# Counting graph edges on TensorE: lanes of ten destinations in place of chunks of 125 edges

## The reference, cut to what matters

```python
src, dst: 20000 edges over N = 1250 nodes, sorted by dst; x: 1250 x 512
# first layer, with h = relu(layernorm(x)), xn = batchnorm(h)
agg = segment_sum(xn[src], dst)                      # neighbours
agg = agg / max(deg, 1)
conv_out = relu(agg @ W_conv + b_conv)
# Performer attention over the first 256 dense rows of h: q, k, v, phi(q), phi(k), kv, z
x = x + batchnorm(conv_out + attention(h) + h)
# second layer, with h = relu(layernorm(x))
agg = segment_sum(h[src], dst)
z = (1 + eps) * h + agg
h = relu(batchnorm(relu(batchnorm(z @ W1 + b1)) @ W2 + b2)); x = x + (z's input h) + h
```

## Time and profile before

| | us |
|---|---|
| median of 3 runs | 365.77 |
| lowest, highest | 365.72, 365.85 |
| span of the profiled execution | 363.9 |
| what the runs' median has beyond that span | 1.87 |
| PE busy in the span | 349.3 |
| DVE busy | 245.2 |
| ACT busy | 181.7 |
| POOL busy | 94.1 |

### The profile page before, as it was taken

How to read it: one execution, slowest core, us unless ns; L and a number is a source line. 1 busy time by engine, 2 the same in 40 slices (tenths; PEclk the granted TensorE clock), 3 DMA queues, 4 the chain that set the end, 5 groups by cost and what they waited for, 6 DMA issues and landing times.

```text
span 363.9 us, 6197 instructions
## 1 busy us (share of the span) xinstructions
PE 349.3 (96%) x2072; PEld 224.6 (62%) x2072; DVE 245.2 (67%) x666; ACT 181.7 (50%) x303; POOL 94.1 (26%) x163
## 2 busy tenths in 40 slices
PE   8999899989999999999998999999999999999994
PEld 4678655757777666767565675455555555565562
DVE  5889999998998995867996886522464453422325
ACT  0548538768477167454437766411533644233132
POOL 8132020000000000100042778722277465101100
PEclk9999999999999999999999999999999999999998
DMA  6990303300000000034900000000000000010223
GB/s 179 283 304 19 119 1 119 118 3 1 3 3 4 3 3 3 3 103 145 263 7 3 0 2 3 2 2 1 2 0 0 2 0 2 0 51 21 70 58 85
DMA packets 13539, 18.05 MB, mean 50 GB/s; under 512 B 1839, under 2 KB 6895, under 8 KB 13491
## 3 DMA queue, kind: packets, MB, share of 16 engines
q1 hardware_dynamic: 12538, 17.21, 16.3%
q10 hardware_dynamic: 953, 0.23, 0.3%
HBM read 14.88 MB, written 2.56 MB: 48 GB/s over the span
## 4 chain that ended last, share of the span: by engine, by line
PE 82%; DVE 6%; ACT 5%; issue 3%; POOL 2%; DMA 1%; DVEq 0%; SPq 0%; ACTq 0%; POOLq 0%
PE bank L1436 78%; PE bank L1466 2%; PE bank L1834 1%; POOL ln_s L491 1%; ACT hn L688 1%; PE bank L1793 1%; DVE st_row L1324 1%; ACT hh L832 1%; ACT sqr L694 1%; DMA edge<-src 1%; DVE x L1387 0%; PE bank L1647 0%; ACT hring L602 0%; DVE aggf L1344 0%; DVE hl L1305 0%
## 5 line engine op out<-in xcount | busy, mean ns | idle before, releaser
L1436 PE MATMUL bank<-AT,hh 125*128 125x400 f16 (+3 forms) x250 | 81.1, 332 | 1.0 <-DVE hl L1305 0.5
L1436 PE MATMUL bank<-AT,hl 125*128 125x400 f16 (+3 forms) x250 | 80.8, 331 | 0.0
L994 DVE TENSOR_SCALAR ring<-iota_code,code 125x250 f16<-125x250 f16 x200 | 46.1, 306 | 1.4 <-issue 1.4
L1436 PEld LDWEIGHTS bank<-AT,hh 125*128 125x128 f16 x250 | 24.1, 97 | 19.2 <-issue 1.1
L1436 PEld LDWEIGHTS bank<-AT,hl 125*128 125x128 f16 x250 | 24.2, 97 | 17.7 <-issue 0.2
L1436 PE MATMUL bank<-ring,S 125*128 125x250 f16 x200 | 33.5, 310 | 0.0
L1436 PE MATMUL bank<-a_hi,w_hi 128*128 128x400 f16 (+1 forms) x96 | 32.6, 339 | 0.0
L1436 PE MATMUL bank<-agg_hi,w_hi 128*128 128x400 f16 (+1 forms) x96 | 32.6, 339 | 0.0
L1436 PE MATMUL bank<-agg_hi,w_lo 128*128 128x400 f16 (+1 forms) x96 | 32.5, 338 | 0.0
L1436 PE MATMUL bank<-a_hi,w_lo 128*128 128x400 f16 (+1 forms) x96 | 32.5, 338 | 0.0
L1436 PE MATMUL bank<-agg_lo,w_hi 128*128 128x400 f16 (+1 forms) x96 | 32.5, 338 | 0.0
(11 more groups left out here) (236 smaller groups left out, 704.2 us busy)
## 6 DMA issues: line engine op xcount, KB each, us to landing
w_s<-w SPq DMA_DIRECT2D x4, 1024.0 KB, 5.0
x_in<-x SPq DMA_DIRECT2D x5, 448.0 KB
x<-x SPq DMA_DIRECT2D x2, 1120.0 KB
out<-x SPq DMA_DIRECT2D x6, 224.0 KB
wB<-wk SPq DMA_DIRECT2D x1, 1024.0 KB, 9.3
wA<-wq SPq DMA_DIRECT2D x1, 1024.0 KB, 14.3
wC<-w_conv SPq DMA_DIRECT2D x1, 1024.0 KB, 16.0
wB<-wv SPq DMA_DIRECT2D x1, 1024.0 KB, 6.0
```

The source lines that it names most:

```text
L994: return dve.tensor_scalar(ring[:, slot, j, a:b], iota_code[0:CH, a:b], code[:, bass.ds(c + j, 1)], float(-CODES * t), ALU.subtract, ALU.i ...
L1436: return pe.matmul(o, l, r, start=start, stop=stop, skip_group_check=True)
```

## The change

A lane is now 10 destinations (`LANE`), so there are 125 lanes and a window is five of them. A lane takes 256 edges from the granule (32 edges) in which it begins, as two products of 128 edges; its codes are 10 destinations x 10 tiles = 100. A window is ten products of 100 columns, two for each lane's own 100 columns of the bank, 1000 columns in all. The edges of every lane are put side by side at the start-up, by PE: `first` marks the row and granule in which each lane begins, and 20 products `edge16` x `first` pick the 256 edges of all 125 lanes for `dst` and `src`. DVE makes codes from them (`lane2`, `code2`), with each value written twice, side by side. The two one-hot instructions of a window read `iota_code` and such pairs. A flag `irregular` is made once in place of the ranges; where it is not 0 (a lane reaches over more than 8 granules, or `dst` is not sorted) all edges are counted again by a loop. In the given inputs the lanes have 127 to 185 edges and reach over 6 granules at most.

The edges now come in three overlapping DMAs for `dst` (SP) and three for `src` (ACT's queue), 384 edges to a row of 125 rows, after two memsets on DVE. ACT turns them to f16. `AT` is evicted with 50 destinations together, from PSUM columns ten apart. The branch for exact counts on DVE and PE (`big_r`) now hangs on the same flag.

```diff
-CH = 125
-NCH = E // CH
-G = 8
-Q = 4
+GRAN = 32
+REACH = 8
+LANE = 10
+LANES = N // LANE
+LPW = W // LANE
+CPL = T * LANE
+CODES = LPW * CPL
+CHUNKS = REACH * GRAN // P
+JOBS = LPW * CHUNKS
-SPARE = {"start": 20, "ranges": 5, "hT0": 3, "hT1": 3, "hT2": 4}
+SPARE = {"start": 14, "firsts": 10, "hT0": 3, "hT1": 3, "hT2": 4}
...
-            return banks[COUNT_BANK[t]][0:L, 0:CODES].rearrange("p (h a b) -> p h a b", h=2, a=T)
+            return banks[COUNT_BANK[t]][0:L, 0:CODES].rearrange("p (d a) -> p a d", a=T)
...
+        EDGE_LOADS = ((0, L - 2, WIDE), (L - 2, 1, 2 * EROW), (L - 1, 1, EROW))
...
         def _(act):
+            act.wait_ge(sem("s_pad"), 2)
+            for rows in EDGE_LOADS:
+                load_edges(act, 1, *rows)
+            for a, name in enumerate(("d_dst", "d_src")):
+                act.wait_ge(sem(name), 16 * len(EDGE_LOADS))
+                act.activation(edge16[:, a, :], edge[:, a, :], ACT.Copy).then_inc(sem("s_edge16"), 1)
...
-                dve.tensor_tensor(S[:, slot], iota_lane[0:CH], a, ALU.is_equal)
...
-                return dve.tensor_scalar(ring[:, slot, j, a:b], iota_code[0:CH, a:b], code[:, bass.ds(c + j, 1)],
-                                         float(-CODES * t), ALU.subtract, ALU.is_equal)
...
+            def one_hots(t):
+                if t >= 2:
+                    dve.wait_ge(sem("s_win"), t - 1)
+                jobs = slice(t * JOBS, (t + 1) * JOBS)
+                for o, n, values in ((S, P, lane2), (ring, CPL, code2)):
+                    shape = [P, JOBS, n // 2, 2]
+                    ins = dve.tensor_tensor(o[:, t % 2].rearrange("p j (q d) -> p j q d", d=2),
+                                            pairs(iota_code[:, 0:n]).unsqueeze(1).broadcast_to(shape),
+                                            values[:, jobs, :].unsqueeze(2).broadcast_to(shape), ALU.is_equal)
+                ins.then_inc(sem("s_hot"), 1)
...
                 if t + 1 < NW:
-                    first_lanes(t + 1)
+                    one_hots(t + 1)
                 if t:
                     low_counts(t - 1)
-                further_chunks(t)
-                if t + 1 < NW:
-                    first_chunks(t + 1)
-                if t + 2 < NW:
-                    load_range(t + 2)
+                further_edges(t)
...
-                if name == "RG":
-                    pe.wait_ge(sem("s_halves"), 1)
...
-            def count(ps, t, j, a, b, start, stop):
-                return mm(ps[:, a:b], S[:, t % 2, :, j], ring[:, t % 2, j, a:b], start, stop)
+            def count(ps, t, j, start, stop):
+                k = j // CHUNKS
+                return mm(ps[:, k * CPL:(k + 1) * CPL], S[:, t % 2, j, :], ring[:, t % 2, j, :], start, stop)
...
-                pe.load([out_r], win[t:t + 1, 1:2])
...
-                for n, j in enumerate(CHUNK_ORDER[:-1]):
-                    if n % Q == 0:
-                        pe.wait_ge(sem("s_hot"), G // Q * t + n // Q + 1)
-                    count(ps, t, j, *CHUNK_COLS[j], n == 0, False)
+                pe.wait_ge(sem("s_hot"), t + 1)
+                for j in range(JOBS - 1):
+                    count(ps, t, j, j % CHUNKS == 0, j % CHUNKS == CHUNKS - 1)
```

More of the change, by code:

```diff
@@ L29 @@
 HB = HID // P
-CH = 125
-NCH = E // CH
-G = 8
-Q = 4
+EROW = E // L
+GRAN = 32
+GPR = EROW // GRAN
+REACH = 8
+WIDE = (GPR - 1 + REACH) * GRAN
 W = 50
 NW = N // W
[L36 to L46, removed]
+LANE = 10
[5 more added lines that the diff above has]
+JOBS = LPW * CHUNKS
+FAR = 2
+PAD_DST = 2000
 COLS = [(0, 450), (450, 400), (850, 400)]
@@ L123, in take @@
         used[bank] += 1
-    take("codes", 2)
-    take("ranges", 3)
+    take("chosen", 2)
+    take("firsts", 3)
     for slot in SLOTS:
@@ L277, in gnn_kernel @@
         hT = place("hT", [P, FB, N], F32, 65)
-        ring = place("ring", [CH, 2, G, CODES], F16, 112.75)
-        S = place("S", [CH, 2, P, G], F16, 128.5)
+        ring = place("ring", [P, 2, JOBS, CPL], F16, 112.75)
+        S = place("S", [P, 2, JOBS, P], F16, 116.75)
+        edge = place("edge", [L, 2, WIDE], I32, 121.75)
+        lane2 = place("lane2", [P, LANES * CHUNKS, 2], F16, 124.75)
+        code2 = place("code2", [P, LANES * CHUNKS, 2], F16, 205.75)
+        below = place("below", [L, LANES, GPR + 1], F16, 125.75)
+        first = place("first", [L, GPR, P], F16, 127.25)
+        src_tile = place("src_tile", [P, CHUNKS * LANES], I32, 129)
+        code_all = place("code_all", [P, CHUNKS * LANES], F32, 130)
+        edge16 = place("edge16", [L, 2, WIDE], F16, 88)
+        fall = place("fall", [L, EROW], F16, 89.5)
+        from_row = place("from_row", [1, LANES + 1], F32, 90)
+        span_row = place("span_row", [1, LANES], F32, 90.5)
         dg = place("dg", [P, 2, MAXN], F32, 134.5)
@@ L410, in _ @@
         def _(sp):
[L411 to L415, removed]
+            sp.wait_ge(sem("s_pad"), 2)
+            for rows in EDGE_LOADS:
+                load_edges(sp, 0, *rows)
             load_x(sp, 0)
@@ L1160, in further_chunks @@
[L1160 to L1173 removed]
+            far = Own(dve, sem("own_far"))
@@ L1586, in attention @@
                         released("P")
-                        pe.load([most_r], most[0:1, 0:1])
                     ps = open_group(pe, name)
@@ new lines, in _ @@
+                pe.wait_ge(sem("s_hot"), t + 1)
+                for j in range(JOBS - 1):
+                    count(ps, t, j, j % CHUNKS == 0, j % CHUNKS == CHUNKS - 1)
+                with pe.If_lt(none_r, flag_r):
+                    count(ps, t, JOBS - 1, False, True).then_inc(sem("s_grp"), 1)
+                    mm(ps[:, 0:CODES], zeros16[0:L, 0:1].broadcast_to([L, P]), iota_code[0:L, :], True, False)
+                    far_ring = ring[0:L, t % 2].rearrange("p (j k) n -> p j (k n)", j=FAR)
+                    with pe.Fori(0, EROW // FAR):
+                        pe.reg_add(seen, seen, 1)
+                        pe.wait_ge(sem("s_hotx"), pe.snap(seen, min_val=1, max_val=1 << 20))
+                        for j in range(FAR):
+                            ins = mm(ps[:, 0:CODES], S[0:L, t % 2, j, :], far_ring[:, j, :], False, False)
+                        ins.then_inc(sem("s_grp"), 1)
+                    mm(ps[:, 0:1], ones16[0:L, :], zeros16[0:L, 0:1], False, True).then_inc(sem("s_win"), 1)
```

286 lines of the change are left out of this document (117 added, 169 removed), and 4 rows, old and new, of tables (LONE_BANKS, SLOTS).

## The result

The changed kernel takes **355.67 us** (median of 4 runs, 355.01 to 358.01), against 365.76 us for the kernel before on the same chip: a ratio of 0.9737, 95% interval 0.9707 to 0.9767, so 10.1 us less by the medians and 9.6 by the ratio. The forecast was 350.3 us, with 347.5 to 353 for its own case and 347 to 355.5 for 8 in 10, so the result lies outside both. The direction and the prices of a window's count and one-hots were right, and the loop gave somewhat more than reckoned; the start was wrong. The profiled span is 354.0 us. One run of experiment 1 (354.53 us) was a slow one, over 1.5% above the fastest of its kernel, and is left out of the figures there; with it the median is 352.29 us.

What follows compares the result with a forecast made beforehand. PE was taken to bound the kernel (busy 349.3 of 363.9 us), with ACT or DVE stretches between. Stages 0.5 + 3.3 + 0 + 3.3 + 0.7 + 7.65 = 15.5 us off 365.77 gave 350.3; own case 347.5 to 353 (0.63), 8 in 10 347 to 355.5.

Steps and rivals of the forecast that it cites:

- Stage 1: Start-up to 22.8 us: 0.5 us gained, 0.26 from dropping the `RG` products and 0.25 for everything else.
- a later start: Rival: the longer edge path makes K0 start 2 us later, giving 352.6 us; chance 0.13.
- ACT's table load: Start-up: the 1.28 us load comes with the edges' copy, no longer ahead of the first `hring`; bound 1 us gain.
- PE's count and DVE's one-hots: Per window: count 0.45 us instead of 1.17; one-hots 0.82 + 0.68 us, with overlap 1.45 instead of 2.49.
- The rule of neighbouring words: DVE one-hots: a repeated f16 pair is one word without its neighbour, so about 2.3 us a window; not taken.
- Stages 2 and 3: 22.8 to 53.5 us: 3.3 us gained, mostly DVE's one-hots; 53.5 to 59.09 us: zero, ACT works in its order.
- Stages 4 and 5: 59.09 to 78.94 us: 3.3 us gained, 0.5 of PE's idle 1.58 remaining; to 88.41 us: 0.7 from window 11.
- Stage 6: 88.41 to 160 us: windows 13 to 24 give 8.65 us, less 1.0 for ACT's `hn` and `kf`: 7.65.
- The new wait behind both one-hots: `s_lo` of t - 1 follows the one-hots of t + 1; a bank 0 count waits for it, and it just holds.
- The rival with slow one-hots: One-hots take 2.3 to 2.7 us a window on DVE: 356.9 us at the upper price, about 354 at 2.3; chance 0.14.
- the slower rival: TensorE's 2.4 GHz level comes much later, at about 38 us instead of 7: 366.6 us or more; chance 0.03.
- The split of the gain: Of PE's 18.1 us over 25 windows, 3.6 and 1 us are lost, and DVE gives back some 2.

Runs made afterwards that it cites:

- experiment 1: Changed kernel with its 123-row edge loads cut into 112 and 11 rows, same bytes: 352.04 us, ratio 0.9588.
- experiment 2: Changed kernel with its 123-row edge loads cut into 120 and 3 rows: 349.92 us, ratio 0.9594.
- experiment 5: Changed kernel with edge loads in 112 + 11 rows and POOL's clearing of `ATlo` moved behind the third row scale: 349.80 us, ratio 0.9551.
- experiment 8: Kernel of experiment 6 with the low counts of window t ahead of the one-hots of t + 1 on DVE: 352.53 us, ratio 0.9621.
- experiment 9: Kernel of experiment 6 with four extra products, 1750 columns in all, ahead of every window's ten on PE: 363.11 us, ratio 0.9922.
- experiment 10: Kernel of experiment 6 with both one-hot instructions reading one repeated f16 element instead of a repeated pair: 360.07 us, ratio 0.9842.
- experiment 6: Changed kernel with edge loads in 120 + 3 rows and POOL's clearing of `ATlo` moved behind the third row scale: 349.72 us, ratio 0.9556.
- experiment 3: Changed kernel with its 123-row edge loads cut into 119 and 4 rows: 354.35 us, ratio 0.9684.
- experiment 11: Kernel of experiment 6 with the first pair of x tiles issued by SP ahead of the edges: 352.10 us, ratio 0.9639.

## Why the prediction was right and wrong

- **Stage 1, the step that failed.** The prediction said: "I take 0.25 of gain for all this beside `RG`; bounds are 1 us of gain (table load) and 2.5 us of loss". The loss was 6.6 us. The view was the right one (the edges' landing at 3.97 us), and a later start was named as a rival, at 352.6 us and 0.13. What failed is its price: the step counted the bytes and the copies in series, and did not ask how a load of 123 rows is served, nor what a late landing does to the clock. 123 rows landed at 11.26 us where 120 took to 5.06, and about 1.5 us of the loss came from the low clock behind PE's idle stretch. With the load cut into 120 + 3 rows and nothing else changed the kernel takes 349.92 us (350.9 by its ratio), against a forecast of 350.3 (experiment 2). That they lie so close is in part luck: the profiled span of that run is 347.2 us where 348.4 were forecast, because from K0 on it gains over 1 us more than reckoned.
- **ACT's table load** did leave its place ahead of the first `hring`: it ran at 2.51 us, and K0 at 14.26 to 14.90 us in the profiles of experiments 2, 5, 8, 9 and 10 is 0.3 to 0.9 us earlier than before. The 0.25 of gain was of the right size there. It is not certain even with the edges in time: in experiment 6 they were there at 5.09 us, x came late, and K0 was at 16.02, 0.9 later than before.
- **PE's count and DVE's one-hots** came out at the forecast numbers (0.46, 0.82 and 0.67 us). The rule of neighbouring words that the prediction weighed, by which the pair would cost 2.3 us a window, does not hold for this operand: the two take 1.49 us. (The 1.73 ns that the prediction took from the Trainium skill is its figure for 4-byte words with a jump of 4 KiB at every element of one source, not for one word read again.) What decides is another rule, which experiment 10 shows with both sides: a repeated single element costs double. The Trainium skill (VectorE: DVE Perf Modes, What auto-detection actually checks) gives it: the fast mode wants 16-bit elements one step apart, and a repeated pair has that, a repeated element does not.
- **Stages 2 and 3:** 5.45 us for 3.55. Stage 3 was right: from `qf` (54.77 before, 55.94 after) to G0 are 4.3 us in both. Stage 2 was reckoned with two windows of one-hots ahead of `qmax`; the tail of a third one lay in that stretch as well, and the chain there alternates between DVE and PE, so that part of the shorter counts came on top. By the chains, `RG` gave 0.4 us, window 1 0.7, and the stretch from the turns at 39.65 us (45.15 after) to `qf` 4.3, where 2.6 were reckoned. How the surplus divides between one-hots and counts was not measured.
- **Stages 4 and 5:** 3.50 and 0.73 us for 3.3 and 0.7; of PE's idle 1.58 us at 77.35, where 0.5 were to remain, 0.2 do. **Stage 6:** 6.97 for 7.65; the loss to ACT's `hn` and `kf` was seen at the right place (98.16 to 108.88 us in the chain), and 1.7 us are lost in this stage, not 1.0. PE itself waits for `kf` for only 0.4 us there (and for 1.1 near 84 us), so the rest of the 1.7 is not accounted for.
- **The new wait behind both one-hots** "just holds": nothing is gained without it. The other order is 2.8 us slower (experiment 8).
- **The rival with slow one-hots** was priced at 356.9 us at the upper price; experiment 10 is that case and takes 360.07 us. What a late DVE costs was undervalued by 3 us.
- **The clock.** It fell, as the slower rival feared, but was back at 1.00 from 17 us on. It cost about 1.5 us (5.16 for 3.65), and the forecast had nothing for it. The rival's own figure does not add up: 350.3 + 15.5 is 365.8, not 366.6.
- **The split of the gain** was right in kind: of 15.5 us the prediction's summary hung all but some 2 on PE's columns (its stages hung 11.2 us on them), and 14.1 us come back with them (experiment 9). But such a split depends on the order of taking away: the slow one-hots alone bring back 10.3 us (experiment 10).

## What to carry to other kernels

When a change alters the shape of a load, look at the number of its rows as well as its bytes: 120 rows landed 5.5 to 6.3 us before 123 here, with the remainder of 3 rows in a transfer of its own. A load that lands later also meets what other engines do at that time, so read the timeline of all engines around the new landing. And where two engines take turns, price their parts together: by the medians a short count with slow one-hots was worth 5.7 us, short one-hots with a long count 2.9, and both together 16.

## What the runs showed of the hardware

- A load of 123 rows of 1.5 KB, issued at 1.35 to 2.09 us, was complete at 11.26 us; as 120 + 3 rows at 4.97 to 5.75 us in five profiles, as 119 + 4 at 6.49, as 112 + 11 at 4.93 and 5.48.
- A DVE copy or scalar instruction from SBUF to SBUF that starts with or inside a POOL memset ends with it: 2.75, 1.73 and 2.85 us for 0.17, 0.17 and 0.29, with a memset of 2.71 us. Instructions with two sources beside the same memset kept their time.
- An f16 operand that repeats one pair runs at 0.53 ns an element, one that repeats a single element at 1.05 (816 and 1481 ns for 1280 elements).
- After PE's idle stretch of 6.9 us the granted clock was 0.50 from 10 to 15 us, after one of 4.0 us 0.50 too (experiment 3), after one of 3.7 us 0.66 on average (experiment 1), after one of 2.8 us 0.72 (experiment 11), and after one of 0.7 us 1.00 (experiment 2). At 0.50 PE's stretch of 36 products took up to 6.37 us, at 1.00 it took 3.65.

The fastest versions are those of experiments 5 and 6, 349.8 us: 4.5% below the kernel before by their ratios (0.9551 and 0.9556), where the change as it was made is 2.6% below it.
